# Two attentions of width 16: maxima transferred from ACT, queries' products four slots earlier, output turnings in slots 7 and 1

## What is computed

```python
def _L3_xattn_ref(Q, K, V, mask, Wq, bq, Wk, bk, Wv, bv, Wo, bo):
    q = (Q @ Wq + bq).reshape(b, sq, H, DHEAD).transpose(0, 2, 1, 3)
    k = (K @ Wk + bk).reshape(b, -1, H, DHEAD).transpose(0, 2, 1, 3)
    v = (V @ Wv + bv).reshape(b, -1, H, DHEAD).transpose(0, 2, 1, 3)
    scores = jnp.einsum('bhqd,bhkd->bhqk', q, k) / np.sqrt(DHEAD).astype(np.float32)
    scores = jnp.where(m == 0, -jnp.inf, scores)
    attn = jax.nn.softmax(scores, axis=-1)
    out = jnp.einsum('bhqk,bhkd->bhqd', attn, v)
    out = out.transpose(0, 2, 1, 3).reshape(b, sq, DM)
    return out @ Wo + bo
x = x + _L0_xattn_ref(ctx_1024, _layernorm(x, axis=-1), ctx_1024, ...)
...
x = x + _L3_xattn_ref(_layernorm(x, axis=-1), ctx_1024, ctx_1024, mask_Bx1xS2_ik0, ...)
```

## The kernel before, in words

| unit | on PE | taken out by | slot before | slot after |
|---|---|---|---|---|
| k, keys, two of a sequence | L1019 | ACT L860 | 0, 4 | 0, 4 |
| q, queries of four sequences, two | L1023 | ACT L860 | 3 | 7 |
| v, values, three, second attention only | L1029 | ACT L865 | 5, 6, 3 | 5, 6, 3 |
| m, the maxima turned | L1035 | ACT L870 | 1 | 1 |
| turn_y, outputs turned | L1040 | DVE L914 and L916 | 6 | 7 |
| turn_n, normalised outputs turned back | L1043 | ACT L872 | 7 | 1 |
| out, product with Wo | L1046 | DVE L922 | 2 | 2 |

## Time and profile before

### The profile page before, as it was taken

The page is one execution under the profiler, slowest core; times in us unless marked ns, Lnnn a source line. Parts: engine busy times, 40 slices in busy tenths (PEclk is TensorE's granted clock), DMA queues, the critical chain, the costliest instruction groups (busy, mean ns, idle before and its releaser), DMA issues. The chain is left out here.

```text
span 2640.4 us, 62412 instructions
## 1 busy us (share of the span) xinstructions
PE 2208.6 (84%) x23896; PEld 1460.3 (55%) x23896; DVE 1561.2 (59%) x3648; ACT 1375.1 (52%) x2919; POOL 954.2 (36%) x1066
## 2 busy tenths in 40 slices
PE   4989399599999999868589999999974992899756
PEld 2556255377777777636356666666652551566533
DVE  3666672566665665456766666666665644555463
ACT  2666363355555555334366666666653652566543
POOL 3443222254444544313323233233313742443043
PEclk8999599799999999959799999999986996999967
DMA  5663361300000000010200000000023215333133
GB/s 121 118 115 65 112 212 35 121 17 10 14 14 14 8 14 2 2 33 1 92 8 14 9 14 10 13 14 8 2 69 101 72 57 119 91 74 74 31 106 107
DMA packets 118579, 139.57 MB, mean 53 GB/s; under 512 B 15072, under 2 KB 107184, under 8 KB 118288
## 3 DMA queue, kind: packets, MB, share of 16 engines
q1 hardware_dynamic: 110900, 115.39, 17.0%
q0 software_dynamic: 7392, 20.19, 2.5%
HBM read 93.25 MB, written 17.47 MB: 42 GB/s over the span
## 5 line engine op out<-in xcount | busy, mean ns | idle before, releaser
L899 DVE TENSOR_REDUCE a_mx<-a_pair 112x2 f32<-112x750 f32 x256 | 238.0, 936 | 191.5 <-PE a_pair L968 191.5
L1207 POOL TENSOR_TENSOR a_kp<-a_kp 125x512 f16<-125x512 f32 x192 | 217.6, 1158 | 259.4 <-ACT a_kp L1298 259.4
L308 POOL TENSOR_SCALAR a_P<-a_P,a_inv 112x375 f32<-112x375 f32 x256 | 148.4, 593 | 447.5 <-DVE a_inv L435 447.5
L430 DVE CUSTOM_DVE_ANT_0 a_masked<-a_s,a_mask_add 112x375 f32<-112x375 f32 x256 | 130.1, 546 | 156.2 <-PE a_s L556 156.2
L837 ACT ACTIVATE a_PT<-a_pair 125x672 f32<-125x672 f32 x256 | 186.2, 730 | 66.6 <-PE a_pair L980 61.9
L346 ACT ACTIVATE a_P<-a_masked,a_least 112x375 f32<-112x375 f32 x256 | 153.5, 601 | 81.7 <-DVE a_least L430 81.7
L520 PE MATMUL a_p<-a_kc,a_wk 128*128 128x375 f16 x768 | 147.9, 329 | 21.2 <-DVE a_k L460 10.2
L1341 DVE SCALAR_TENSOR_TENSOR a_k<-a_p,a_k 128x375 f16<-128x375 f32 x128 | 69.3, 547 | 139.2 <-ACT a_k L1254 139.2
L534 PE MATMUL a_p<-a_wv,a_kc 128*125 128x512 f16 x576 | 142.4, 383 | 10.5 <-DVE a_k L460 10.4
L1298 ACT CAST a_kp<-a_kp 125x512 f16<-125x512 f32 x192 | 110.4, 617 | 76.4 <-DVE a_kp L1360 76.4
L1440 PE MATMUL a_p<-a_kc,a_wk 128*128 128x375 f16 x768 | 142.2, 326 | 5.4 <-POOL a_kc L1199 5.4
(11 more groups left out here) (420 smaller groups left out, 5258.8 us busy)
## 6 DMA issues: line engine op xcount, KB each, us to landing
a_kc<-in_ctxT SPq DMA_DIRECT2D x64, 375.0 KB, 4.1
a_k<-a_k_parts SPq DMA_DIRECT2D x192, 93.8 KB
w_stage<-in_L_ffn_W SPq DMA_DIRECT2D x32, 512.0 KB
w_stage<-in_L_ffn_ew SPq DMA_DIRECT2D x16, 512.0 KB, 6.6
w_stage<-expert_rows SPq DMA_DIRECT2D x16, 448.0 KB, 7.6
a_v_in_sb<-in_ctx SPq DMA_DIRECT2D x16, 375.0 KB
a_q<-a_q_parts SPq DMA_DIRECT2D x48, 112.0 KB, 3.7
w_stage<-in_L_ffn_W SPq DMA_DIRECT2D x16, 256.0 KB, 3.9
```

Source lines behind the costliest of these rows:

```text
L308: pool.tensor_scalar(P[:, p % 4, r, :], P[:, p % 4, r, :], inv[:, p % 4, r:r + 1], 1.0, ALU.mult, ALU.mult).then_inc(P_done, 1)
L430: dve.tensor_tensor_reduce(masked[:, p % 2, r, :], s_bank[0:S, r, 0:SK], mask_add[:, b % 2, :], 1.0, 3e38, ALU.add, ALU.min, least[:, p % ...
L899: dve.tensor_reduce(mx[:, b % 2, 2 * pair:2 * pair + 2], pair_bank[slot["score", p]][0:S, :, 0:SK], AX.X, ALU.max).then_inc(max_done, 1)
L1207: pool.tensor_tensor(kp16[:, LO, j, hf, r, :, :].rearrange("p c m -> p (c m)"), kp[:, n % 4, :], kp16[:, HI, j, hf, r, :, :].rearrange("p ...
```

## The change

It does three things in `narrow_attention_phase`. The two DMAs of the maxima are issued by ACT, right behind its own copy to `mT` (slot 1), instead of by SP in slot 2; ACT waits first for the copy to be complete. The queries' units move from steps -29 and -21 to -33 and -25, that is from slot 3 to slot 7. turn_y moves from slot 6 to slot 7 and turn_n from slot 7 to slot 1; out stays in slot 2. No instruction is added or taken away, and no size changes.

```diff
--- before.py
+++ after.py
@@ -608,9 +608,9 @@
     SLOTS = ((HI, HI), (LO, HI), (HI, LO))
     N_STACK = 2 * len(SLOTS) + (2 if mask is not None else 0)
     N_CONST = 2 * (2 if mask is not None else 1)
-    FIRST, LAST = -29, 8 * (B - 1) + LAG + 13
-    K_AT, Q_AT, V_AT, M_AT = (-16, -12), (-29, -21), (5, 6, 11), 9
-    TURN_Y, TURN_N, OUT = LAG + 9, LAG + 10, LAG + 13
+    FIRST, LAST = -33, 8 * (B - 1) + LAG + 13
+    K_AT, Q_AT, V_AT, M_AT = (-16, -12), (-33, -25), (5, 6, 11), 9
+    TURN_Y, TURN_N, OUT = LAG + 10, LAG + 12, LAG + 13
 
     def units_at(s):
 
@@ -760,13 +760,6 @@
                         sp.dma_start(q[64 * r + 16 * i:64 * r + 16 * i + 16, g % 2, :, :],
                                      q_parts[:, part, r, :]).then_inc(q_in[g % 2], 16)
 
-                def stack_maxima(b):
-                    g, t = divmod(b, GT)
-                    sp.wait_ge(emptied, number["m", b, 0] + 1)
-                    for r in range(2):
-                        sp.dma_start(q[64 * r + KS:64 * r + KM, g % 2, :, t * S:(t + 1) * S],
-                                     mT[16 * r:16 * r + 16, b % 2, :]).then_inc(m_in[b % 2], 16)
-
                 for s in steps:
                     for b in range(B):
                         t = s - 8 * b
@@ -780,8 +773,6 @@
                         if t == -33 and b >= 3:
                             sp.wait_ge(kc_split, b - 2)
                             load_context(sp, b)
-                        if t == 10:
-                            stack_maxima(b)
 
             @block.gpsimd
             def _(pool):
@@ -837,6 +828,13 @@
                     act.activation(PT[:, p % 4, :, :], pair_bank[slot["turned", p]][0:KP, :, 0:KT * S],
                                    ACT.Exp).then_inc(exp_done, 1)
 
+                def stack_maxima(b):
+                    g, t = divmod(b, GT)
+                    act.wait_ge(emptied, number["m", b, 0] + 1)
+                    for r in range(2):
+                        act.dma_start(q[64 * r + KS:64 * r + KM, g % 2, :, t * S:(t + 1) * S],
+                                      mT[16 * r:16 * r + 16, b % 2, :]).then_inc(m_in[b % 2], 16)
+
                 def high_context(b):
                     act.wait_ge(kc_in[b % 3], 16 * (b // 3 + 1))
                     if b >= 4:
@@ -890,6 +888,8 @@
                     for unit in units_at(s):
                         if unit[0] in ("k", "q", "v", "m", "turn_n"):
                             evacuate(unit)
+                        if unit[0] == "m":
+                            stack_maxima(unit[1])
 
             @block.vector
             def _(dve):
```

## The result

The changed kernel takes 2674.9 us (median of four runs, 2665.7 to 2685.2) against 2632.0 for the kernel before beside it: ratio 1.0166, interval 1.0139 to 1.0192. That is slower, as forecast, but by 43 us and not by 19, and outside the range. The profiled execution took 2683.63 us.

What follows compares the result with a forecast made beforehand. PE sets the pace, busy 11.01 of 11.21 us in a first-attention round. Terms 26.9 + 8.1 + 0.8 - 17.8 + 2.0 + 15.9 - 16.6 = +19.3 us on the 2631.1 median give 2650.4 us; range 2622 to 2670.

Steps and rivals of the forecast that it cites:

- slot 1, turn_n ahead of the maxima: Slot 1, both attentions: the maxima's matmul waits for ACT's copy of turn_n; +0.96 us in 28 rounds, +26.9 us.
- keys behind turn_y, slot 0: Slot 0: keys wait until DVE has emptied the bank of turn_y; +0.37 us in 22 rounds, +8.1 us.
- slots 6 and 7, first attention: First attention: slot 7's turned scores must wait for slot 6's maximum; +0.06 us in 14 rounds, +0.8 us.
- slot 6, second attention: Slot 6 without turn_y, so v no longer waits for DVE: -1.48 us; with slot 7's +0.21, -17.8 us over 14 rounds.
- queries in slot 7: Slot 7, first attention: queries' unit waits behind turn_y, 0.5 us more, four times, +2.0 us; second attention taken as equal.
- ACT held by its two issues: Slots 2 and 3: ACT's DMA issues delay its exponential and the weighing; +0.53 us in 30 rounds, +15.9 us.
- the landing of the maxima: First attention: all four stalls on the maxima's transfers and three slow-clock stretches go, -16.6 us; bounds 0 and -16.6.
- the second rival: First attention: the maxima's transfers land as late as before, stalls and slow clock stay; +16.6, 2667.0 us; chance 0.17.
- half clock in the looser rounds: Sign of being wrong: stalls with half clock appearing in the new, looser rounds; no size given.
- The queries' start: Start of each attention: one queries' unit now precedes the first scores; 1.71 us each, +-3.4 in all, taken as 0.
- The rival that ACT is not held: Slot 2: ACT's exponential starts as now despite the issues, the +15.9 falls away; 2634.5 us; chance 0.15.
- The rival that PE's waits for ACT are absorbed: Slots 7, 0 and 1: PE's new waits replace its waits for ACT's exponentials; sum -6.7, 2624.4 us; chance 0.13.

Runs made afterwards that it cites:

- e1: Kernel before with only the maxima's transfers issued by ACT instead of SP: 2649.3 us, ratio 1.0068.
- e5: Kernel before with the first attention's context block load issued in slot 2, behind the maxima's transfers, instead of slot 7: 2626.4 us, ratio 0.9982.
- e13: Changed kernel with the first attention's values' loads cut to one partition from the third sequence on (output wrong): 2665.4 us, ratio 1.0085.
- e15: Changed kernel with the first attention's queries' stack of the last two groups cut to an eighth or less (output wrong): 2674.5 us, ratio 1.0131.
- e3: Kernel before with only the queries' units moved to slot 7, maxima still on SP: 2630.4 us, ratio 1.0000.
- e2: Kernel before with only turn_y moved to slot 7 and turn_n to slot 1: 2643.3 us, ratio 1.0056.
- e7: Kernel before with the values put ahead of turn_y where they share a slot (second attention, slot 6): 2629.1 us, ratio 0.9986.
- e17: Changed kernel with six groups of unread keys' matmuls added in the first attention's last rounds: 2671.5 us, ratio 1.0148.
- e16: Changed kernel run again unchanged, against the kernel before: 2674.2 us, ratio 1.0157.

## Why the prediction was wrong, and where it was right

Each price against the slots of the undisturbed rounds (my working is above, with the earlier trace rows):

| step | forecast, a round | measured |
|---|---|---|
| slot 1, turn_n ahead of the maxima | +0.96 | 1.21 to 2.18: +0.97 |
| keys behind turn_y, slot 0 | +0.37 | 1.59 to 1.95: +0.36 |
| slots 6 and 7, first attention | +0.06 | 2.89 to 3.00: +0.11 |
| slot 6, second attention | -1.48 | 2.83 to 1.34: -1.49 |
| slot 7, second attention | +0.21 | 1.52 to 1.76: +0.24 |
| queries in slot 7 | +0.5 | 1.93 to 2.49 for a queries' unit: +0.56 |
| ACT held by its two issues | +0.53 | +0.45 first, +0.56 second (e1) |
| the landing of the maxima | -16.6 in all | 7.9 us of waits became 15.0 |

**The step that failed** is the last of the sum: "I take all four stalls as gone, with the three slow stretches", 16.6 us. The bound at the other end, 0, was the right one. I put the stalls down to what stands ahead in SP's queue. e1 has nothing ahead in ACT's and waits 8.9 us for 7.9; e5 takes the context's load out from ahead of them and waits 8.3. e13 to e15 show for the steady rounds that it is the sum of what is in flight, and q10's empty 6.4 us that a queue of its own doesn't help. The queries' move, whose effect on the stalls I had as none, makes them longer (23.6 us in e3). Without the failed step my sum is +35.9, 2667.0 us, which is the second rival; two of after's four runs lie at 2666. It had 0.17 of the chance and should have had most: both the higher DMA share of the stretch with the stalls (0.62 for 0.43) and the Trainium skill's section on issuing engines spoke for it, and against it stood only an argument on order.

The other 8 us to the median (2674.9 less 2667.0) are in no term of the sum. The profile, of one of the two longer executions, has them and more at the end of the first attention: the tail takes 4 us more even at a clock near before's (e13 and e15: 35.3 and 34.9 us at 0.80 and 0.82, before 30.8 at 0.83), and half clock in the last rounds and the tail adds the rest. The prediction's last sentence named half clock in the looser rounds as a sign of being wrong and gave it no price. Its cause and its part in the median are open. The prices of the parts, each within 0.1 us a round, were read from rows and are no luck. That the direction came out right is theirs too: they outweigh the stalls.

The queries' start, taken as 0, gives 8 us in the first two rounds (e3) and loses them in stalls. The price of a queries' unit in slot 7 came, but not for my reason alone: e3, where it stands behind turn_n and turn_y hasn't moved, pays 2.48 us for it as after pays 2.49. That ACT's exponential starts behind its DMA rows, the keys' wait for VectorE, L1035's 0.43, the missing wait of L1029 in slot 6, and rounds of 13.1 and 14.8 came as written. The clock of 1.00 from 80 us did not: it was at half from 80.9 to 91.2 and in seven later stretches.

The rival that ACT is not held is refuted: the exponential starts 0.10 us behind the second issue, after 1.41 us idle, though the matmuls of its turned scores had ended at 249.61, 1.2 us earlier. What the Trainium skill's Sequencer Loop (Advanced Engine Details and Errata) says of reading and queueing other instructions meanwhile did not let an exponential start during ACT's DMA issues here. The rival that PE's waits for ACT are absorbed is refuted too: e2, with the turnings alone, is slower by 0.0056.

## What to carry to other kernels

A small transfer that others wait for was not made early here by issuing it from another engine: ask how much is in flight when it is issued. Thinning any one of the large ones cleared the waits of the steady rounds; moving them in the order gained little or lost. Two units that share a bank and a slot cost what the first one's emptying takes, here 0.4 to 1.5 us a round for units whose own work was unchanged, and their order is worth testing (e7: 0.36 us a round from one sort). And where a change only adds waits to a full engine, look at the clock as well, above all in the rounds where other work has already run out, and in more than one execution.

## What was not expected of the hardware

- Transfers on ACT's own queue started no packet for 6.4 us, while the DMA engines' share was 0.41 for five of these, and PE's wait for them ended 11.3 us after the issue. The packets then took 4 us more. Undisturbed, all were over within 3 us of the issue.
- Issuing slows down with the load: three queries' stacks held SP for 3.56 us instead of 1.9, six keys' stacks for 5.76 instead of 3.75.
- ACT pays 0.64 us for each small DMA that it issues (1.28 for two), as SP does (1.34 for two), and starts nothing behind them meanwhile.
- One and the same stretch of code, with nearly the same number of matmuls, took 34.9 to 35.8 us at a clock of 0.80 to 0.85 (e13, e15, e17) and 41.8 and 43.7 at 0.58 and 0.50 (after, e16).
- Longer rounds can take up stalls: with the turnings moved, ten rounds that each grew by 1.41 us made a stretch only 3.4 us longer (e2).
